# Between two layers: the last x1 addition in three parts, and low halves 2 to 7 on GpSimd beside its gathers

## Time and profile before

| | |
|---|---|
| median of 3 runs | 1157.14 us (1156.62 to 1157.24) |
| the profiled execution | 1156.27 us |
| its span, first to last instruction | 1154.5 us |
| mean granted TensorE clock | 0.983 |
| busy: PE, PE weight loads, DVE, ACT, POOL | 93%, 78%, 48%, 26%, 13% |
| chain that ended last, by engine | PE 85%, DVE 5%, POOL 4%, issue 2%, ACT 2%, DMA 1% |

### The profile page before, as it was taken

How to read it: one execution, slowest core, us unless ns; L and a number is a source line. 1 busy time by engine, 2 the same in 40 slices (tenths; PEclk the granted TensorE clock), 3 DMA queues, 4 the chain that set the end, 5 groups by cost and what they waited for, 6 DMA issues and landing times.

```text
span 1154.5 us, 13705 instructions
## 1 busy us (share of the span) xinstructions
PE 1069.3 (93%) x5431; PEld 901.7 (78%) x5434; DVE 548.8 (48%) x660; ACT 303.2 (26%) x485; POOL 154.4 (13%) x194
## 2 busy tenths in 40 slices
PE   0799999999999999999789999999999999988774
PEld 0679888888888888888778888888888888877651
DVE  7544554334344444344663343343443343356786
ACT  1222221211212121211442121122132132124675
POOL 7900000000000000000141001001010010023425
PEclk9999999999999999999899999999999999998897
DMA  2766310010101000020321112021021021032103
GB/s 99 239 236 208 107 44 12 1 54 0 54 0 54 0 33 21 0 91 1 121 71 43 41 55 82 27 81 55 27 82 55 27 96 40 27 110 73 47 1 146
DMA packets 26655, 73.92 MB, mean 64 GB/s; under 512 B 5442, under 2 KB 5634, under 8 KB 26498
## 3 DMA queue, kind: packets, MB, share of 16 engines
q1 hardware_dynamic: 20994, 48.35, 11.8%
q0 software_dynamic: 5632, 25.17, 7.1%
HBM read 69.15 MB, written 4.36 MB: 64 GB/s over the span
## 4 chain that ended last, share of the span: by engine, by line
PE 85%; DVE 5%; POOL 4%; issue 2%; ACT 2%; DMA 1%; SPq 0%; DVEq 0%; ACTq 0%; POOLq 0%
PE ps_gu L137 18%; PE ps_gu L138 18%; PE ps_gu L139 18%; PE ps_d L137 8%; PE ps_d L138 8%; PE ps_d L139 8%; PE ps_t L137 1%; PE ps_t L139 1%; PE ps_t L138 1%; POOL theta L435 1%; POOL mag L435 1%; PE ps_gu L836 1%; DVE h_lo L1570 1%; PE ps_t L727 1%; POOL trig L431 1%
## 5 line engine op out<-in xcount | busy, mean ns | idle before, releaser
L137 PE MATMUL ps_gu<-a_hi,gu_hi 128*128 128x512 f32 x800 | 316.3, 395 | 2.2 <-DVE a_lo L1288 2.2
L138 PE MATMUL ps_gu<-a_lo,gu_hi 128*128 128x512 f32 x800 | 314.1, 393 | 0.0
L139 PE MATMUL ps_gu<-a_hi,gu_lo 128*128 128x512 f32 x800 | 313.2, 391 | 0.0
L137 PEld LDWEIGHTS ps_gu<-a_hi,gu_hi 128*128 128x128 f32 x800 | 151.9, 190 | 31.6 <-DVE a_lo L1288 2.3
L139 PEld LDWEIGHTS ps_gu<-a_hi,gu_lo 128*128 128x128 f32 x800 | 151.4, 189 | 32.2
L138 PEld LDWEIGHTS ps_gu<-a_lo,gu_hi 128*128 128x128 f32 x800 | 151.8, 190 | 28.7
L1424 DVE TENSOR_TENSOR s_act<-s_act,ps_gu 128x512 f32<-128x512 f32 x44 | 30.3, 688 | 195.0 <-PE ps_gu L139 194.8
L1312 DVE TENSOR_TENSOR s_act<-s_act,ps_gu 128x512 f32<-128x512 f32 x56 | 38.5, 687 | 152.9 <-PE ps_gu L139 152.9
L307 POOL DMA_INDIRECT lr_raw<-in_tab_l,rows x48 | 45.8, 955 | 370.4 <-PE ps_t L727 346.3
L137 PE MATMUL ps_d<-h_hi,dn_hi 128*128 128x512 f32 x224 | 87.6, 391 | 0.0
L139 PE MATMUL ps_d<-h_hi,dn_lo 128*128 128x512 f32 x224 | 87.2, 389 | 0.0
(11 more groups left out here) (239 smaller groups left out, 1730.8 us busy)
## 6 DMA issues: line engine op xcount, KB each, us to landing
raw<-in_w SPq DMA_DIRECT2D x26, 768.0 KB, 5.6
toep_hi<-krev_hi SPq DMA_DIRECT2D x16, 512.0 KB, 5.8
toep_lo<-krev_lo SPq DMA_DIRECT2D x16, 512.0 KB, 7.0
acc<-in_x_t SPq DMA_DIRECT2D x4, 1024.0 KB, 10.6
out<-x1b SPq DMA_DIRECT2D x16, 256.0 KB, 2.0
w_all<-in_wq SPq DMA_DIRECT2D x1, 1024.0 KB, 8.3
raw<-in_wq SPq DMA_DIRECT2D x4, 256.0 KB, 4.2
lr_raw<-in_tab_l,rows POOLq DMA_INDIRECT x48, 4.1
```

The costliest lines, as they stand in the source:

```text
L137: pe.matmul(out_ap, st_hi, mv_hi, start=start, stop=False, skip_group_check=skip)
L138: pe.matmul(out_ap, st_hi, mv_lo, start=False, stop=False, skip_group_check=skip)
L139: return pe.matmul(out_ap, st_lo, mv_hi, start=False, stop=stop, skip_group_check=skip)
```

## The change

- The last x1 addition has three parts: batches 0 to 7, 8 to 15, and 16 to 63. The first two count s_evk, the third s_ev.
- ACT writes a_hi(0) and a_hi(1) as their parts are done, and only then waits for the third part.
- DVE writes a_lo(0) between the second and the third part. a_lo(1) stays behind the two dn_lo. Both count s_x1l.
- a_lo of groups 2 to 7 leaves DVE's steps. POOL computes it in its gather loop, behind the gather of the same group and ahead of the next gather, after a wait for a_hi of the group. It counts the new semaphore s_x1p, and PE's matmuls of groups 2 to 7 wait for that.
- POOL's wait before it clears x1b is on both counts.

The diff:

```diff
@@ -160,7 +160,7 @@
         s_g, s_u, s_silu, s_mul, s_hh, s_hl, s_d = ([sem(f"{n}{f}") for f in range(2)] for n in (
             "s_g", "s_u", "s_silu", "s_mul", "s_hh", "s_hl", "s_d"))
 
-        s_ev, s_evk, s_x1h, s_x1l = sem("s_ev"), sem("s_evk"), sem("s_x1h"), sem("s_x1l")
+        s_ev, s_evk, s_x1h, s_x1l, s_x1p = (sem(n) for n in ("s_ev", "s_evk", "s_x1h", "s_x1l", "s_x1p"))
         s_wall, s_wsum, v_zero = sem("s_wall"), sem("s_wsum"), sem("v_zero")
 
         c_a, c_tr, c_ah, c_al, c_tp, c_tm, c_th, c_tl = ([sem(f"{n}{i}") for i in range(2)] for n in (
@@ -507,6 +507,10 @@
                     if g >= 2:
                         pool.wait_ge(c_tr[g % 2], g // 2)
                     gather(pool, ar_raw[:, g % 2], tab_a, rows0[:, g:g + 1]).then_inc(c_a[g % 2], 16)
+                    if g >= 2:
+                        pool.wait_ge(s_x1h, g + 1)
+                        pool.tensor_tensor(x_group(a_lo, g), x_group(x1b, g), x_group(a_hi, g).bitcast(F32),
+                                           ALU.subtract).then_inc(s_x1p, 1)
 
 
                 def step(t):
@@ -520,7 +524,8 @@
                 for i in range(2):
                     pool.wait_ge(c_tr[i], NG // 2)
                 step(0)
-                pool.wait_ge(s_x1l, NG)
+                pool.wait_ge(s_x1l, 2)
+                pool.wait_ge(s_x1p, NG - 2)
                 pool.memset(x1b[:], 0.0).then_inc(v_zero, 1)
                 for i in range(2):
                     pool.wait_ge(c_tp[i], NG // 2)
@@ -693,8 +698,10 @@
                         at = bass.ds(i * (2 * GT) + u * GT, GT)
                         for w in range(2):
                             for k in range(KB):
-                                if w == 0 and k == 0:
-                                    pe.wait_ge(s_x1l, 2 * i + (u + 1))
+                                if w == 0 and k == 0 and first:
+                                    pe.wait_ge(s_x1l, u + 1)
+                                elif w == 0 and k == 0:
+                                    pe.wait_ge(s_x1p, 2 * i + (u - 1))
                                 last = mm3(pe, t_bank[u][:, w], ar_hi[:, u, w * KB + k], ar_lo[:, u, w * KB + k],
                                            a_hi[:, k, at], a_lo[:, k, at], start=(k == 0), stop=(k == KB - 1), skip=True)
                         last.then_inc(c_tp[u], 1)
@@ -971,10 +978,10 @@
 
                     act.activation(x_group(a_hi, g), x_group(x1b, g), ACT.Copy).then_inc(s_x1h, 1)
 
-                act.wait_ge(s_evk, 1)
-                x1_high(0)
+                for g in range(2):
+                    act.wait_ge(s_evk, g + 1)
+                    x1_high(g)
                 act.wait_ge(s_ev, M1)
-                x1_high(1)
 
                 def split(u, n):
                     act.wait_ge(c_tr[u], n + 1)
@@ -1287,6 +1294,12 @@
                     hv = a_hi4[:, :, h0:h0 + 2].rearrange("p k h b -> p h k b").bitcast(F32)
                     dve.tensor_tensor(a_lo4[:, :, h0:h0 + 2].rearrange("p k h b -> p h k b"),
                                       ytmp[:, q % 2].rearrange("p h (k b) -> p h k b", k=KB), hv, ALU.subtract).then_inc(s_ylo, 1)
+
+                def x1_low(g):
+
+                    dve.wait_ge(s_x1h, g + 1)
+                    dve.tensor_tensor(x_group(a_lo, g), x_group(x1b, g), x_group(a_hi, g).bitcast(F32),
+                                      ALU.subtract).then_inc(s_x1l, 1)
 
                 def masked(t):
 
@@ -1345,9 +1358,12 @@
                         ps_heads = ps_d[:].rearrange("p k (h b) -> p k h b", b=BATCH)
                         hs = slice(t * HPT, (t + 1) * HPT)
                         if last_chunk and t == NT - 1:
-                            for sl, s_done in ((slice(0, GB), s_evk), (slice(GB, BATCH), s_ev)):
+                            for b, n in ((0, GB), (GB, GB), (2 * GB, BATCH - 2 * GB)):
+                                sl = slice(b, b + n)
                                 dve.tensor_tensor(x1b4[:, :, hs, sl], acc4[:, :, hs, sl], ps_heads[:, :, :, sl],
-                                                  ALU.add).then_inc(s_done, 1)
+                                                  ALU.add).then_inc(s_evk if n == GB else s_ev, 1)
+                                if b == GB:
+                                    x1_low(0)
                         elif last_chunk:
                             dve.tensor_tensor(x1b4[:, :, hs], acc4[:, :, hs], ps_heads, ALU.add).then_inc(s_ev, 1)
                         else:
@@ -1373,13 +1389,6 @@
                 chunk(NC0 - 1, False, True)
 
 
-                def x1_low(g):
-
-                    dve.wait_ge(s_x1h, g + 1)
-                    dve.tensor_tensor(x_group(a_lo, g), x_group(x1b, g), x_group(a_hi, g).bitcast(F32),
-                                      ALU.subtract).then_inc(s_x1l, 1)
-
-                x1_low(0)
                 x1_low(1)
 
                 def split(u, n):
@@ -1400,11 +1409,6 @@
                         at = bass.ds(i * (2 * GT) + u * GT, GT)
                         dve.tensor_tensor(t_lo[:, :, at], tm[:, u].rearrange("p (a n) -> p a n", a=2),
                                           t_hi[:, :, at].bitcast(F32), ALU.subtract).then_inc(c_tl[u], 1)
-                        if not last_pair:
-                            ahead = bass.ds(i * (2 * GT) + (2 + u) * GT, GT)
-                            dve.wait_ge(s_x1h, 2 * i + (u + 3))
-                            dve.tensor_tensor(a_lo[:, :, ahead], x1b[:, :, ahead], a_hi[:, :, ahead].bitcast(F32),
-                                              ALU.subtract).then_inc(s_x1l, 1)
 
                 pair(0, False)
                 with dve.Fori(1, NG // 2 - 1) as i:
```

## The result

The changed kernel takes 1168.43 us at the median of four runs (1166.55 to 1169.53) against 1157.19 for the kernel before: 11.2 us later, where 11.5 had been forecast. The ratio is 1.011 with a 95% interval of 1.0095 to 1.0125, which is 12.7 us (11.0 to 14.5).

A forecast was written before the change was run, and what follows sets the result against it. TensorE, busy 93% of the span, bounds the kernel, so its idle time counts. Group 7 7.3 us later plus 4.2 for clock falls makes 11.5 us; with 1156.27 profiled and 0.87 to the median, 1168.7 us, range 1162.5 to 1173.

The forecast's parts named there:

- The head: x1 addition in three parts between the layers: group 0 starts 3.0 us earlier, group 1 3.6 us earlier.
- Off DVE: Low halves 2 to 7 leave DVE, six times 1.22 us: worth about 0.2 us a group, not 1.2.
- The low half on POOL: Price of one low half of 1024 elements on POOL: 2.45 us, with ends 2.4 and 2.94.
- The chain: Mask, a_hi, POOL low half, gather, transposes, matmuls: 13.1 us per pair of groups; group 7 7.3 us later, clock up.
- The falls of the clock: PE gaps before groups 2, 4 and 6 lower its clock three times, 1.4 us each, 4.2 us together.
- The second and third gap: PE standing still before groups 4 and 6: about 4.6 us each.
- the low end: Low end of the range: clock up, landings at 3.8 us, another microsecond for handovers: +5.4, 1162.5 us.
- Behind group 7: POOL's layer 1 gathers and clearing of x1b and td last to about 613, needed near 616.5: stay hidden.
- the clock did not stay up: Rival: PE's clock stays up through the three gaps, giving +7.3, 1164.4 us; chance 0.15.
- the faster case: Rival: gathers, judged at gather 3's landing, stay covered, keeping the head's lead: -4.8, 1152.3 us; chance 0.04.
- POOL and DVE did not hold each other up: Rival: DVE's t_lo and POOL's low half hold each other up, three times 0.8 us: +13.9, 1171.1 us; chance 0.08.
- The case of no difference: Rival: the losses vanish into slack behind the layers, 1157.1 us; chance 0.03.

The follow-up runs named there:

- two ahead: Changed kernel, with POOL issuing the gather of group g+2 ahead of the low half of group g; ratio 0.9988 to the kernel before, stretch 43.0 us.
- the head alone: Kernel before, with only the x1 addition in three parts and a_lo(0) moved; low halves 2 to 7 stay on DVE; ratio 0.998, stretch 43.2 us.
- the run with filled gaps: Changed kernel plus 18 useless products on PE behind groups 1, 3 and 5; ratio 1.0061 to the kernel before, stretch 53.4 us.
- the two reordered runs: Changed kernel, POOL issuing the gather of group g+2, or only g+1, ahead of low half g; ratios 0.9988 and 0.9978 to the kernel before.
- the run with the low half twice: Changed kernel, with low halves of groups 2, 4 and 6 computed twice in a row on POOL; ratio 1.0159 to the kernel before, stretch 66.5 us.
- the run with the wait alone: Kernel before with the new head, low halves on DVE, POOL only waiting for a_hi(g) ahead of gather g+1; ratio 1.0071, stretch 55.7 us.

## Why the prediction was right

- **The head** was right. Counted from the first addition, group 0 starts at 3.10 us instead of 6.05 and group 1 at 8.15 instead of 11.63: 2.95 and 3.5 us earlier, 3.0 and 3.6 forecast. The clock fell in the first gap here too, and tm(0) followed a_lo(1) at once, as costed.
- **Off DVE** was right in kind: with the order mended, tm follows tm in 4.48 us (two ahead) where the head alone takes 4.84, so 0.36 us a group instead of the 0.2 forecast. ACT and DVE still set this pace: with two ahead, ar_lo on DVE waits 1.0 us for ar_hi in each step.
- **The low half on POOL** was costed at 2.45 us and took 2.34 to 2.38. The estimate from the Trainium skill's GPSIMD Engine Reference (Elementwise — side-by-side cycle accounting) was 2.25; the measurement lies between the two.
- **The chain** was right: 13.1 us for a pair of groups was forecast, and the run with filled gaps, whose clock stays up, shows 12.96, 12.95 and 13.43 from tm to tm (565.78, 578.74, 591.69, 605.12). With the clock up 7.3 us in all were forecast, and 7.2 measured (53.4 against 46.2).
- **The falls of the clock** were three, as forecast, and were mis-sized: 1.4 us each, 4.2 together, against 1.3, 2.5 and 1.4, together 5.1. The cap of 1.8 us was read from group 0, whose transposes had run before its gap; behind the new gaps the transposes run first and take 1.97 us instead of 1.03. The second group ran at half clock for 5.4 us (589.03 to about 594.5) where the forecast went by the 2.8 us seen in the tail. For these 2.8 us the forecast worked out 1.0, which is too little, since the 4.99 us of group 0 end with matmuls at full clock: starts of matmuls 0.21 us apart at half clock and 0.12 at full give 1.2.
- **Two slips beside the sum.** The second and third gap were put at 4.6 us and were 5.37 and 5.96, the third behind a gather that landed after 4.6 us instead of 4.0. And three landings of 3.8 us take 0.6 off 7.3, so the low end, with the further microsecond off, comes to +5.7 and not +5.4.
- **Behind group 7** the clearing of x1b stayed hidden, as forecast: DVE's first work on layer 1's hidden values waits for PE in both traces, at 609.16 before and at 621.23 after, where the clearing had ended at 618.9:

```profile
617.04 1.82 POOL L533 MEMSET td<- 128x2048 f32 x1
```

```profile
621.23 0.69 DVE L1428 TENSOR_TENSOR s_act<-s_act,ps_gu 128x512 f32<-128x512 f32 x1 [4.54 <-PE ps_gu L139]
```

The number is closer than its working. The terms add up to 11.5 us and the stretch shows 12.7; what is missing is nearly all in the falls of the clock, 4.2 against the 5.5 that filling the gaps gave back. That the medians come within 0.3 us of the forecast is in part luck, with four runs that scatter over 3 us.

The rivals: the clock did not stay up. The gathers were not covered, and the two reordered runs show how much of the faster case was to be had by covering them, 3.2 us of the 4.8 named by the stretch, and less by their times (1.4 and 2.5 us). In the changed kernel POOL and DVE did not hold each other up: its low halves keep to 2.34 to 2.38 us, its gathers to 0.95 to 0.96 and t_lo to 0.69. They missed each other by 0.3 us, as forecast (t_lo ends at 567.81, the low half starts at 568.12), and the run with the low half twice shows that the hold-up is real where they meet. The case of no difference is ruled out by the interval of 11.0 to 14.5 us.

Taken apart by the runs, with the clock up: the head -3.0; the wait for a_hi ahead of a gather about +2.4 (the worked-out 45.6 against 43.2); the low half in the chain about +7.8 (53.4 against 45.6); and the clock +5.5 on top (58.9 against 53.4).

## What to carry to other kernels

When work is moved onto an engine that issues DMAs, ask what each DMA behind it used to wait for, and what it waits for now: a transfer with 13 us of cover lost it all by standing behind a 2.4 us operation and the wait of that operation. Put the issue ahead of the work, as far as the buffers allow, and look at what is issued last on the queue as well. A gap that opens on TensorE costs its length and the lowered clock behind it, here 5.1 us behind gaps of 17.0 in all.

## What the runs showed of the hardware

An indirect gather that POOL begins to issue 0.1 to 0.25 us after DVE has started a subtraction of two tensors in SBUF takes 1.80 to 1.94 us to issue instead of 0.94, and ends about 0.8 us behind that subtraction (five times of five in the run with the wait alone). The gather shown from the run with the low half twice also ends 0.8 us behind a t_lo (575.01 and 574.18). A gather that waits for the end of the subtraction takes 0.94 again. DVE's side of the first row, from the run with the wait alone:

```profile
569.11 1.22 DVE L1410 TENSOR_TENSOR a_lo<-x1b,a_hi 128x1024 fp32r<-128x1024 f32 x1 [0.26 <-ACT a_hi L996]
```

In the kernel before, a gather that was issued first (570.56, with a t_lo of two SBUF inputs starting at 570.84) kept its 0.94 us, so there the one that started first was not held. Which part of an issue is held, no run shows. The Trainium skill's SBUF — State Buffer (Who interferes with whom) infers that such a VectorE instruction does not stall descriptor generation. These runs differ, for indirect gathers at least, and the measurement decides.
